# Attention beside routing: GpSimd's row transfers of a group dealt 5, 2 + 1 + 4 and 4 over three batches, and the first batch's matmuls in another order

## The chip, the cores and the metric

The kernel runs on one core of a Trainium2 chip. The core has TensorE (PE, matrix products into the eight PSUM banks), VectorE (DVE), ScalarE (ACT), GpSimd (POOL), SyncE (SP, which issues DMAs) and 16 DMA engines. Each engine takes its own instructions in order, and engines wait for one another by semaphores. The metric is the time of one execution in microseconds, the median over runs. The profile is of a single execution.

## The reference

One launch computes four residual blocks on 16 sequences of 256 tokens with 128 features:

```python
x = x + s4d_block(layernorm(x))      # long convolution by FFT, then a norm
x = x + mixture(layernorm(x))        # 8 experts, the best 2 of them, and a shared one; hidden 512
x = x + attention(layernorm(x))      # 16 heads of 8 features, causal, with a slope per head
x = x + mixture(layernorm(x))        # the same weights again

logits = q @ k.T * scale + slopes * (j - i);  masked to j <= i
out = softmax(logits) @ v @ Wout

logits = xf @ gate_w + gate_b;  top_w, top_i = top_k(logits, 2);  gw = softmax(top_w)
out = sum_e combine[:, e] * (gelu(xf @ w1[e] + b1[e]) @ w2[e] + b2[e]) + shared(xf)
```

## The kernel before

The kernel has four stages, with a barrier of all engines between them: the front (convolution, gating), the attention stage (which first finishes the experts of the first mixture), the shared expert of the second mixture, and the routed experts of it. The change touches the attention stage alone.

**The attention stage** works through 16 batches (sequences) of four quarters (`G` = 0 to 3, four heads each). Every engine has a function `quarter_of(b, G)`, called for all batches in order, so the order of each engine's work is written out by hand. A batch is spread over several steps: in step `b` TensorE computes the scores of batch `b` (`scores`, line 1994 and 1998, with masks on 1947), the maxima of batch `b + 1` (`maxima`, in two tiles, lines 1953 and 1970), the projections of `b + 3`, and the end of `b - 1` and `b - 2`. Quarters are numbered `x = 4 b + G`.

- `maxima(y, tile)` writes banks 2 and 3; VectorE reduces them (`reduce`, line 2227) before the next maxima may write them. The reduced rows are turned, copied by ScalarE (line 2145) and written into the query rows by small DMAs of SyncE (`spread_m`, line 1859). `scores` of quarter 0 and 2 wait for these.
- `scores(x)` writes banks 5 to 7 when the exponential before it is through (`exps`). ScalarE's `expo` (line 2150) reads them.
- `weigh(x)` (lines 2029, 2030) multiplies the exponentials with the values, into bank 4. `expo(x)` waits for `weigh(x - 2)`.
- In step 0 the last of the first mixture's rows come in (`middle`: ScalarE line 1697, turned by TensorE, line 1712).

**The second mixture's routing** runs beside it. When batch `c` is complete, VectorE takes its statistics (line 2249); GpSimd makes the mean and scale of them (`batches.statistics`, lines 1111 to 1121); ScalarE normalises in step `c + 3`, quarter 2, ahead of its exponential (line 1134); GpSimd splits the rows (`batches.rows`, lines 1126 and 1127), and SyncE turns them (line 1143). Four batches make a group of eight tiles of 128 rows. VectorE chooses the experts and places, and GpSimd sends each tile's rows to a DRAM buffer `slots` by indirect DMAs, one for each tile and choice: eight for the first choice (`dispatch_first`, line 1058), eight for the second (`dispatch_second`, line 1071), which first need the index column of the row rewritten (line 1067). Two groups are sent in this stage, group 0 in GpSimd's turns `c` = 7, 8, 9 and group 1 in 11, 12, 13; the other two are sent in the next stage. The second choice of a half (four tiles) waits until the first choice of that half has landed.

GpSimd's loop over `c` takes, in order, the statistics, the places (`place_on_pool`), the row split and the transfers. Its next turn's statistics stand behind these transfers.

Of the kernel before, what the change touches and what calls it, by code (L numbers as in the profile page):

```python
# [51 lines left out]
GRP = 8  # L52
# [1677 lines left out]
def attention_stage(nc, t):  # L1730
# [13 lines left out]
    with ExitStack() as ctx:  # L1744
# [50 lines left out]
        def after(eng, s, n):  # L1795

            if n > 0:
                eng.wait_ge(s, n)

        assert at[0] + ROUTE_WORDS <= ARENA - BACK_WORDS  # L1800
        route = route_program(nc, t, sem, t.arena[:, at[0]:])
# [3 lines left out]
        def batch(c):  # L1805
            return 0 <= c < NB

        def quarter(x):
            return 0 <= x < LAST
# [65 lines left out]
        @block.gpsimd  # L1875
        def _(pool):
            words = [v.rearrange("p s G n -> p (s G n)").bitcast(F32) for v in QPAD]
            for v in (*words, V32[0], V32[1], LATER_ROWS, EARLIER_ROWS, LATER, EARLIER):
                nc.gpsimd.memset(v, 0.0).then_inc(cleared, 1)
            pool.wait_ge(cleared, 9)  # L1880
            for v in V32:
                nc.gpsimd.memset(v[:, :, :, 8:9], 1.0).then_inc(masks, 1)

            for rows, base in ((LATER_ROWS, HALF), (EARLIER_ROWS, HALF - 1)):
                nc.gpsimd.affine_select(out=rows, in_=rows, compare_op=ALU.not_equal, fill=1.0, base=base,
                                        pattern=[[-1, 2 * P]], channel_multiplier=1).then_inc(masks, 1)

            nc.gpsimd.affine_select(out=LATER, in_=LATER, compare_op=ALU.is_ge, fill=-1.0e30, base=0,
                                    pattern=[[0, 2], [1, P]], channel_multiplier=-1).then_inc(masks, 1)

            nc.gpsimd.affine_select(out=EARLIER, in_=EARLIER, compare_op=ALU.is_ge, fill=-1.0e30, base=-1,
                                    pattern=[[0, 2], [-1, P]], channel_multiplier=1).then_inc(masks, 1)
            pool.wait_ge(masks, 6)
            for a in range(2):
                first, at_a = slice(HALF * a, HALF * a + 1), HALF * a
                nc.gpsimd.memset(LATER_ROWS[first, at_a + HALF:at_a + HALF + 1], 0.0).then_inc(masks, 1)
                nc.gpsimd.memset(LATER_ROWS[first, at_a + P:at_a + P + HALF], 1.0).then_inc(masks, 1)
                nc.gpsimd.memset(EARLIER_ROWS[first, at_a:at_a + HALF], 1.0).then_inc(masks, 1)
                nc.gpsimd.memset(LATER[first, :, at_a:at_a + HALF], -1.0e30).then_inc(masks, 1)
            pool.wait_ge(masks, 14)  # L1900
            routed.gpsimd(pool)
            for k in range(len(PIECES)):
                middle.root(pool, k)
            route.clear(pool)
            for c in range(NB - 1):
                pool.wait_ge(row_stats, c + 1)
                batches.statistics(pool, c)
                for g in range(SENT_IN_ATTENTION):
                    if c == 4 * g + 7:
                        route.place_on_pool(pool, g)  # L1910
                batches.rows(pool, c)
                for g in range(SENT_IN_ATTENTION):
                    if c == 4 * g + 7:
                        route.dispatch_first(pool, g, range(0, GRP // 2))
                    if c == 4 * g + 8:
                        route.dispatch_first(pool, g, range(GRP // 2, GRP))
                        route.dispatch_second(pool, g, (0,))
                    if c == 4 * g + 9:
                        route.dispatch_second(pool, g, (1,))
            route.sent_all(pool, SENT_IN_ATTENTION)  # L1920

        @block.tensor
        def _(pe):
# [20 lines left out]
            def mask_later(out, a, half, start):  # L1944

                first = HALF * (a + 1 - half)
                pe.matmul(out[:, :, HALF * half:HALF * half + HALF], LATER_ROWS[PAIR[a], first:first + P],  # L1947
                          LATER[PAIR[a], :, HALF * a:HALF * a + HALF], start=start, stop=False, skip_group_check=True)
# [33 lines left out]
            def scores(x):  # L1982

                c, G = divmod(x, HG)
                if G % 2 == 0:
                    pe.wait_ge(mrow_in[G // 2], 32 * (c + 1))
                if x == 0:
                    pe.wait_ge(middle.low, 4)
                after(pe, exps, x)
                early = [ps[5 + a].rearrange("p (h t n) -> p h t n", t=TPB, n=P)[:, :, 0] for a in range(2)]  # L1990
                late = [ps[7][:, SEQ * a:SEQ * a + SEQ].rearrange("p (h n) -> p h n", n=P) for a in range(2)]

                def early_scores(a):
                    return pe.matmul(ps[5 + a], KST[c % 3][PAIR[a], G, 0:P], QPAD[c % 3][PAIR[a], :, G, :], start=False,  # L1994
                                     stop=True, skip_group_check=True)

                def late_scores(a):
                    return pe.matmul(ps[7][:, SEQ * a:SEQ * a + SEQ], KST[c % 3][PAIR[a], G, P:2 * P],
                                     QPAD[c % 3][PAIR[a], :, G, P:2 * P], start=False, stop=True, skip_group_check=True)
                mask_later(late[0], 0, 0, True)  # L2000
                mask_later(early[1], 1, 0, True)
                mask_later(late[0], 0, 1, False)
                mask_later(early[1], 1, 1, False)
                late_scores(0).then_inc(st_mm, 1)
                early_scores(1)
                mask_later(early[0], 0, 0, True)
                mask_later(early[0], 0, 1, False)
                pe.wait_ge(st_mm, 3 * x + 1)
                mask_later(late[1], 1, 0, True)
                mask_later(late[1], 1, 1, False)  # L2010
                early_scores(0).then_inc(st_mm, 1)
                late_scores(1).then_inc(st_mm, 1)
# [44 lines left out]

            def quarter_of(b, G):
                x = HG * b + G
                if quarter(x):  # L2060
                    scores(x)
                if quarter(x + 4):
                    maxima(x + 4, 0)
                if quarter(x - 1):
                    weigh(x - 1)
                if G == 3:
                    if gate_group(b) is not None:
                        for c in range(4 * gate_group(b), 4 * gate_group(b) + 4):
                            batches.landed(pe, c)
                        after(pe, mrow_set, min(2 * b + 3, 2 * NB))  # L2070
                        route.gate(pe, gate_group(b), ps[0])
                    if rank_group(b) is not None:
                        after(pe, mrow_set, min(2 * b + 3, 2 * NB))
                        route.rank(pe, rank_group(b), ps[0])
                if quarter(x + 5):
                    maxima(x + 5, 1)
                if G == 0:
                    if batch(b - 2):
                        turn_out(b - 2)
                    if batch(b + 3):  # L2080
                        project(b + 3)
                if G == 1 and batch(b - 2):
                    project_out(b - 2)
                if G == 2:
                    if batch(b + 1):
                        pe.wait_ge(vset, b + 2)
                        turn_maxima(b + 1, 0)
                    if batch(b - 1):
                        turn_back(b - 1, 0)
                if G == 3:  # L2090
                    if batch(b + 1):
                        after(pe, mrow_set, 2 * b + 3)
                        if gate_group(b) is not None:
                            route.logits_taken(pe, gate_group(b))
                        if rank_group(b) is not None:
                            route.ranks_taken(pe, rank_group(b))
                        turn_maxima(b + 1, 1)
                    if batch(b - 1):
                        turn_back(b - 1, 1)
                if b == -1 and G == 0:  # L2100
                    middle.turn(pe, 2)
                    middle.turn(pe, 3)
                if b == 0:
                    middle.turn(pe, 4 + G)
                if G == 1 and batch(b + 1):
                    values(b + 1)

# [370 lines left out]
```

## Time and profile before

| | |
|---|---|
| median of 3 runs | 870.53 us (869.16 to 872.47) |
| the profiled execution | 869.57 us, span 867.8 us |
| busy: TensorE, VectorE, GpSimd, ScalarE | 616.0, 618.4, 458.5, 438.3 us |
| row transfers in all | 128 (64 of each choice), 32 of them in the attention stage |
| steps of batches 0 to 15 in attention | from 411.7 to about 625 us |

Times in the rows are from the span's start. The median of the runs is 0.96 us above the profiled execution's own time, and its span is 1.8 us below that. A row of windows gives the stretch and its length, then the busy time of TensorE (PE), its weight loads (PEld), VectorE, ScalarE and GpSimd with their instructions, the granted clock as a share of full speed, the share of the DMA engines' time and GB/s. A row of a timeline gives start, duration, engine, line, operation, result and operand with their shape. Where an engine's row ends in square brackets, it had stood idle for so long before it, and the bracket names what ended the wait.

### The profile page before, as it was taken

To read this page: it belongs to the slowest core of one execution; us is meant where nothing else is said; L and a number is where in the kernel's file an instruction comes from. 1 tells how busy PE (TensorE), PEld (TensorE's weight loads), DVE (VectorE), ACT (ScalarE), POOL (GpSimd) and SP (SyncE) were. 2 spreads that over 40 slices of the span, in tenths; PEclk is the share of its full clock that TensorE was granted. 3 is DMA by queue.
4 is the path that set the end of the run, shared out by engine and by line. 5 is a ranking of instruction groups with operands and counts; after the bars stand their busy time and mean duration, and the time that the engine had idled before them with its cause. 6 is when DMAs were issued, how large, how long until landed. Compare 5 with 4: busy or idle time off the path is not lost. (4 is left out here: it accounts for less than half of the span.)

```text
span 867.8 us, 21824 instructions
## 1 busy us (share of the span) xinstructions
PE 616.0 (71%) x7762; PEld 451.0 (52%) x7762; DVE 618.4 (71%) x1397; ACT 438.3 (51%) x873; POOL 458.5 (53%) x591
## 2 busy tenths in 40 slices
PE   0569975780079999225799999989714795999950
PEld 0354433560069999212566666555402574999940
DVE  6997887683048888287688889888513873888846
ACT  5634457760035555171766676666603332555524
POOL 1238758887547777510002223464764880777760
PEclk9968987995579999755899999999956997999985
DMA  9610002351144464242122233342111512545418
GB/s 284 151 38 1 0 8 67 71 90 50 37 74 90 98 99 88 86 166 62 45 87 71 80 98 88 82 116 55 42 33 29 86 32 47 93 101 100 89 32 285
DMA packets 131850, 70.51 MB, mean 81 GB/s; under 512 B 89535, under 2 KB 118725, under 8 KB 131746
## 3 DMA queue, kind: packets, MB, share of 16 engines
q1 hardware_dynamic: 121042, 50.46, 25.1%
q0 software_dynamic: 9088, 16.88, 7.0%
q10 hardware_dynamic: 1616, 1.77, 0.7%
q8 instruction: 67, 1.10, 0.5%
q14 instruction: 37, 0.30, 0.1%
HBM read 26.61 MB, written 30.50 MB: 66 GB/s over the span
## 5 line engine op out<-in xcount | busy, mean ns | idle before, releaser
L1500 ACT ACTIVATE ARENA<-banks,ARENA 128x256 f32<-128x256 f32 x312 | 122.3, 476 | 97.1 <-PE banks L1460 94.6
L2227 DVE TENSOR_REDUCE ARENA<-banks 128x4 f32<-128x1024 f32 (+1 forms) x128 | 122.8, 959 | 32.5 <-PE banks L1970 29.5
L1458 PE MATMUL banks<-ARENA,W1H 128*128 128x256 f16 x312 | 87.2, 279 | 58.4 <-DMA ARENA<-slots 57.6
L1472 PE MATMUL banks<-W2L,ARENA 128*128 x624 | 110.0, 219 | 2.7 <-DVE ARENA L1513 2.3
L1473 PE MATMUL banks<-W2H,ARENA 128*128 x624 | 109.7, 219 | 0.1
L1474 PE MATMUL banks<-W2H,ARENA 128*128 x624 | 109.7, 219 | 0.0
L2150 ACT ACTIVATE ARENA<-banks 128x1536 f32<-128x1536 f32 x64 | 92.6, 1447 | 24.2 <-PE banks L1994 24.1
L1448 POOL DMA_INDIRECT expert_out_g<-ARENA x78 | 78.0, 999 | 46.6 <-issue 26.2
L1448 POOL DMA_INDIRECT expert_out_f<-ARENA x78 | 81.1, 1040 | 33.6 <-issue 23.9
L1532 DVE TENSOR_TENSOR ARENA<-ARENA 128x1024 f16<-128x1024 f32 x78 | 95.6, 1226 | 2.7
L1058 POOL DMA_INDIRECT slots<-ARENA,PLACE x64 | 77.0, 1204 | 26.0 <-issue 17.5
L1071 POOL DMA_INDIRECT slots<-ARENA,PLACE x64 | 77.5, 1211 | 19.1 <-issue 14.6
L1459 PE MATMUL banks<-ARENA,W1H 128*128 128x256 f16 x312 | 87.1, 279 | 0.0
L1460 PE MATMUL banks<-ARENA,W1L 128*128 128x256 f16 x312 | 87.1, 279 | 0.0
L1530 DVE CAST ARENA<-ARENA 128x1024 f16<-128x1024 f32 x78 | 55.2, 707 | 37.1 <-ACT ARENA L1500 36.6
L1458 PEld LDWEIGHTS banks<-ARENA,W1H 128*128 x312 | 31.3, 100 | 63.5 <-issue 59.3
L1472 PEld LDWEIGHTS banks<-W2L,ARENA 128*128 128x128 f16 x624 | 61.0, 98 | 4.7 <-issue 3.7
L1473 PEld LDWEIGHTS banks<-W2H,ARENA 128*128 128x128 f16 x624 | 61.0, 98 | 1.8 <-issue 0.3
L1474 PEld LDWEIGHTS banks<-W2H,ARENA 128*128 128x128 f16 x624 | 61.0, 98 | 0.0
L488 PE MATMUL banks<-XN,ARENA 128*128 128x512 f32 x64 | 33.6, 685 | 34.0 <-ACT XN L395 29.6
L1953 PE MATMUL banks<-ARENA 64*128 64x128 bf16 x512 | 37.7, 227 | 20.9 <-DVE ARENA L2227 13.4
L1947 PE MATMUL banks<-ARENA 64*128 64x128 bf16 x512 | 47.4, 222 | 5.7 <-ACT ARENA L2150 3.7
(324 smaller groups left out, 1731.3 us busy)
## 6 DMA issues: line engine op xcount, KB each, us to landing
spread<-ARENA SPq DMA_DIRECT2D x96, 64.0 KB
ARENA<-expert_out_f SPq DMA_DIRECT2D x8, 512.0 KB, 6.5
ARENA<-spread SPq DMA_DIRECT2D x16, 256.0 KB, 3.0
ARENA<-spread SPq DMA_DIRECT2D x32, 128.0 KB, 2.8
ARENA<-expert_out_g SPq DMA_DIRECT2D x8, 512.0 KB, 6.6
XT<-in_w SPq DMA_DIRECT2D x10, 256.0 KB, 7.7
slots<-EMPTY SPq DMA_DIRECT2D x16, 129.0 KB
ARENA<-in_w SPq DMA_DIRECT2D x8, 256.0 KB, 6.9
```

What stands on the lines that cost most here:

```text
L1071: nc.gpsimd.indirect_dma_start(xs, bass.IndirectOffsetOnAxis(ap=t.PLACE[:, 1, i:i + 1], axis=0), ROWI[:, i, :], None).then_inc(sent[h], 16)
L1448: nc.gpsimd.indirect_dma_start(yo, bass.IndirectOffsetOnAxis(ap=target, axis=0), Y[i % 4][:, h], None, bounds_check=2 * NT * P - 1, oob_is ...
L1458: pe.matmul(out, t.W1H[:, e, ms], XST[i][:, 0], start=True, stop=False)
L1459: pe.matmul(out, t.W1H[:, e, ms], XST[i][:, 1], start=False, stop=False)
L1460: ins = pe.matmul(out, t.W1L[:, e, ms], XST[i][:, 0], start=False, stop=True)
L1472: pe.matmul(out, hh, t.W2L[:, e, m, :], start=(m == 0), stop=False)
L1473: pe.matmul(out, hh, t.W2H[:, e, m, :], start=False, stop=False)
L1474: ins = pe.matmul(out, hl, t.W2H[:, e, m, :], start=False, stop=(m == MT - 1))
L1500: ins = nc.scalar.activation(HF[i % 2][:, m], UP[i % 2][:, m], ACT.Gelu, bias=BIAS[i % 4][:, m:m + 1], scale=1.0 / WS)
L1532: dve.tensor_tensor(H16[i % 4][:, 1], HF[i % 2], H16[i % 4][:, 0], ALU.subtract).then_inc(split, 1)
L2150: nc.scalar.activation(PR[x % 2], t.psum_all[:, 5:8, :], ACT.Exp, scale=1.0 / LOGIT).then_inc(exps, 1)
L2227: dve.tensor_reduce(MX[:, G // 2, tile, :, :, G % 2].rearrange("p s a -> p a s"), src, AX.X, ALU.max).then_inc(m_red, 1)
```

## The change

GpSimd's eight first-choice transfers of a group were dealt four and four over two turns, each after the row split, and the second choices four and four over the second and third turn. Now the first turn sends five; the second sends two between the statistics and the row split, one after the row split, and then the second choices of the first half; the third turn is as before.

On TensorE, in the steps up to batch 0 (`full` is false), a quarter begins with the first maxima and only then computes the scores, and the weighting of the quarter before comes at the end, before the values. From batch 1 on the order is the old one.

```diff
                 for g in range(SENT_IN_ATTENTION):
                     if c == 4 * g + 7:
                         route.place_on_pool(pool, g)
+                    if c == 4 * g + 8:
+                        route.dispatch_first(pool, g, range(5, 7))
                 batches.rows(pool, c)
                 for g in range(SENT_IN_ATTENTION):
                     if c == 4 * g + 7:
-                        route.dispatch_first(pool, g, range(0, GRP // 2))
+                        route.dispatch_first(pool, g, range(0, 5))
                     if c == 4 * g + 8:
-                        route.dispatch_first(pool, g, range(GRP // 2, GRP))
+                        route.dispatch_first(pool, g, range(7, GRP))
                         route.dispatch_second(pool, g, (0,))
                     if c == 4 * g + 9:
                         route.dispatch_second(pool, g, (1,))
...
                 x = HG * b + G
-                if quarter(x):
+                full = b > 0
+                if full and quarter(x):
                     scores(x)
                 if quarter(x + 4):
                     maxima(x + 4, 0)
-                if quarter(x - 1):
+                if not full and quarter(x):
+                    scores(x)
+                if full and quarter(x - 1):
                     weigh(x - 1)
...
                 if b == 0:
                     middle.turn(pe, 4 + G)
+                if not full and quarter(x - 1):
+                    weigh(x - 1)
                 if G == 1 and batch(b + 1):
                     values(b + 1)
```

On GpSimd, at the first group's turns 7 and 8, the difference reads as follows (1058 is a first-choice transfer, 1111 and on the statistics, 1126 and 1127 the row split):

```order
-L1058 DMA slots<-ARENA,PLACE 36608x129 x4
...
-L1126 CAST ARENA<-XN 128x2x128
-L1127 TENSOR_TENSOR ARENA<-XN,ARENA 128x2x128
-L1058 DMA slots<-ARENA,PLACE 36608x129 x4
+L1058 DMA slots<-ARENA,PLACE 36608x129 x5
...
+L1121 TENSOR_SCALAR NRM<-NRM 128x2
+L1058 DMA slots<-ARENA,PLACE 36608x129 x2
+L1126 CAST ARENA<-XN 128x2x128
+L1127 TENSOR_TENSOR ARENA<-XN,ARENA 128x2x128
+L1058 DMA slots<-ARENA,PLACE 36608x129
```

Four transfers moved: one into the turn before, two ahead of the row split, and one stays behind it; the four second choices follow as they did.

On TensorE, batch 0, from the turn of the late rows that ends quarter 2 (line 1712) into quarter 3, before:

```order
L1712 MATMUL banks<-ID,XN 128x128 x4
L1947 MATMUL banks<-ARENA 128x2x64 x4
L1998 MATMUL banks<-ARENA 128x256
L1994 MATMUL banks<-ARENA 128x512
...
L1953 MATMUL banks<-ARENA 128x2x64 x4
L1970 MATMUL banks<-ARENA 128x128 x4
L2029 MATMUL banks<-ARENA 32x256
L2030 MATMUL banks<-ARENA 32x128
...
L1953 MATMUL banks<-ARENA 128x2x64 x4
L1970 MATMUL banks<-ARENA 128x256 x4
```

and now (its line numbers are two higher):

```order
L1712 MATMUL banks<-ID,XN 128x128 x4
L2031 MATMUL banks<-ARENA 32x256
L2032 MATMUL banks<-ARENA 32x128
...
L1955 MATMUL banks<-ARENA 128x2x64 x4
L1972 MATMUL banks<-ARENA 128x128 x4
L1949 MATMUL banks<-ARENA 128x2x64 x4
L2000 MATMUL banks<-ARENA 128x256
L1996 MATMUL banks<-ARENA 128x512
...
L1955 MATMUL banks<-ARENA 128x2x64 x4
L1972 MATMUL banks<-ARENA 128x256 x4
```

The weighting of quarter 1 (2029, 2030) stood ahead of the second maxima of quarter 2 and now closes quarter 2; the one of quarter 2, shown in the first block, moves behind the second maxima of quarter 3; and the first maxima (1953, 1970 at 128x128) stand ahead of the scores.

## Rows read from the trace of the kernel before

**Rows 1.** The page, the chain that ended last: shares of the span.

```profile
POOL 7%; issue 5%; DVE 2%; DMA 1%; ACT 0%; POOLq 0%; PE 0%; SPq 0%; DVEq 0%; ACTq 0%
```

**Rows 2.** Windows, first exponential to first exponential: batches 8, 10 and 12.

```profile
522.10:534.84 12.74, 12.56 (x208) 7.87 (x210) 11.71 (x28) 9.05 (x14) 3.70 (x13) 1.00 0.30 85
...
547.96:561.93 13.97, 12.45 (x210) 7.88 (x204) 10.98 (x22) 9.05 (x14) 9.16 (x23) 1.00 0.35 99
...
575.40:589.86 14.46, 12.27 (x204) 7.67 (x200) 11.30 (x27) 9.04 (x13) 10.74 (x21) 1.00 0.38 107
```

**Rows 3.** Timeline of GpSimd: start, duration, engine, line, operation.

```profile
566.28 0.22 POOL L1121 TENSOR_SCALAR NRM<-NRM 128x2 f32<-128x2 f32 x1
568.83 0.40 POOL L1126 CAST ARENA<-XN 128x256 f16<-128x256 f32 x1 [2.33 <-ACT XN L1134]
...
570.25 1.09 POOL L1058 DMA_INDIRECT slots<-ARENA,PLACE  x1 [0.29 <-POOL ARENA L1127]
571.65 0.95 POOL L1058 DMA_INDIRECT slots<-ARENA,PLACE  x1 [0.31 <-issue]
...
580.38 0.21 POOL L1111 TENSOR_TENSOR NRM<-RSTATS 128x2 f32<-128x2 f32 x1
```

**Rows 4.** Timelines of ScalarE and TensorE in batch 12.

```profile
581.09 0.38 ACT L2139 ACTIVATE ARENA<-banks 128x256 f32<-128x256 f32 x1 [0.89 <-PE banks L1941]
583.69 0.88 ACT L1134 ACTIVATE XN<-RES,NRM 128x128 f32<-128x128 f32 x2 [2.21 <-POOL NRM L1121]
...
585.95 0.29 PE L1947 MATMUL banks<-ARENA 64*128 64x128 bf16 x4 [1.98 <-ACT ARENA L2150]
```

**Rows 5.** Timelines of SyncE's DMA issues and of TensorE's first scores.

```profile
531.58 3.57 SPq L1859 DMA_DIRECT2D ARENA<-ARENA  x4
553.75 3.82 SPq L1842 DMA_DIRECT2D spread<-ARENA  x6
557.62 3.21 SPq L1859 DMA_DIRECT2D ARENA<-ARENA  x4
566.86 4.24 SPq L1842 DMA_DIRECT2D spread<-ARENA  x6
580.36 4.62 SPq L1842 DMA_DIRECT2D spread<-ARENA  x6
586.18 3.98 SPq L1859 DMA_DIRECT2D ARENA<-ARENA  x4
...
533.92 0.29 PE L1947 MATMUL banks<-ARENA 64*128 64x128 bf16 x4
561.01 0.29 PE L1947 MATMUL banks<-ARENA 64*128 64x128 bf16 x4 [1.34 <-DMA ARENA<-ARENA]
588.95 0.29 PE L1947 MATMUL banks<-ARENA 64*128 64x128 bf16 x4
```

**Rows 6.** Timelines of GpSimd and VectorE at the end of the stage.

```profile
615.53 0.20 POOL L1111 TENSOR_TENSOR NRM<-RSTATS 128x2 f32<-128x2 f32 x1
619.69 0.40 POOL L1126 CAST ARENA<-XN 128x256 f16<-128x256 f32 x1 [0.98 <-ACT XN L1134]
631.23 0.21 POOL L1111 TENSOR_TENSOR NRM<-RSTATS 128x2 f32<-128x2 f32 x1
646.69 0.65 POOL L1127 TENSOR_TENSOR ARENA<-XN,ARENA 128x256 f16<-128x256 f32 x1
...
625.70 0.48 DVE L2249 BATCH_NORM_STATS2 RSTATS<-RES 128x6 f32<-128x128 f32 x2
```

**Rows 7.** TensorE in batch 0, and a window with the granted clock.

```profile
420.08 0.28 PE L1953 MATMUL banks<-ARENA 64*128 64x128 bf16 x4 [1.00 <-DVE ARENA L2227]
425.78 0.28 PE L1978 MATMUL banks<-ID,ARENA 128*16 128x128 f16 x2 [1.78 <-ACT ARENA L2139]
427.12 0.29 PE L1947 MATMUL banks<-ARENA 64*128 64x128 bf16 x4 [0.47 <-ACT ARENA L2150]
...
427.00:429.00 2.00, 1.88 (x24) 1.29 (x28) 0.97 (x2) 1.77 (x5) 0.00 (x0) 0.59 0.01 2
```

## The prediction

> **What bounds the kernel now.** I read the page first, then the attention stage (409 to 652 us) batch by batch, because both edits lie there. The chain that ended last [rows 1] is GpSimd's issue of the last mixture's results; it starts only at 723.6 us, so an earlier end of what lies before it moves it whole. I follow a batch by the start of its first exponential. An undisturbed batch lasts 12.74 us, with TensorE busy for 12.56 of it; batch 10 lasts 13.97 and batch 12 14.46, both at the full clock, with TensorE busy for about as long as ever [rows 2]. So TensorE, in a tight exchange with VectorE and ScalarE, is the bound, and these two batches hold waits.
>
> *Batch 12's wait.* GpSimd issues eight row transfers in batch 11, from 570.25 us, and can begin the statistics of batch 9 only when they are out, at 580.38; they take 3.3 us [rows 3]. ScalarE stood idle 2.21 us before normalising with them: it was free at 581.48 (581.09 + 0.39) and started at 583.69. The exponential behind it came late, and TensorE's next scores waited 1.98 us for that [rows 4].
>
> *Batch 10's wait.* The scores that open a batch need the row of maxima, which SyncE writes with small DMAs. In a quiet batch SyncE begins these at 531.58 and the scores start at 533.92, 2.34 us later. Where four row transfers have been going out since 556.28, SyncE begins at 557.62 and the scores start at 561.01, 3.39 us later, 1.34 of it an idle wait for that DMA [rows 5]. In batch 12 transfers and SyncE's DMAs went out together, from 586.2, and the scores started at 588.95 without a wait: the ScalarE stall had given the DMA time [rows 5].
>
> *The end of the stage.* From 615.53 to 647.34 us GpSimd never waits for VectorE: it is behind. Batch 12's statistics follow the transfers without idle, and batch 13's start at 631.23 though VectorE had finished its part at about 626.1 (625.70, two of 0.24). Its only idle there is 0.98 us for ScalarE's normalisation, ahead of each pair of row copies; the last copy ends at 647.34, its transposes follow, and then all engines meet [rows 6].
>
> **Part 1: the dealing, first group (batches 10 to 12).** A transfer costs 0.95 us and 0.30 until the next, 1.26 in step, and 1.39 for the first after other work [rows 3]. Five instead of four: the fourth ended at 560.21 + 0.95 = 561.16, the fifth at 562.42, before the next statistics at 563.32: covered by 0.9 us. Then two ahead of the row copies: statistics end at 566.50; two take 0.29 + 1.09 + 0.30 + 0.96 = 2.64, to 569.14. The copies started at 568.83, so they are 0.35 late (their transposes were issued at 575.81, so nothing waits). One more and four: copies end 570.3, the single transfer at 571.7, the counter 0.15, and four at 5.1 end at 576.95. That is 3.4 us sooner than 580.37. Batch 9's statistics, whose input came at 576.72, then end at 580.2, 1.3 us before ScalarE wants them. ScalarE's wait of 2.21 goes, and with it TensorE's of **1.98 us** [rows 4].
>
> What is late next: the DMA of the maxima. Without the stall TensorE would want to open batch 13 at 588.95 − 1.98 = 586.97. SyncE cannot begin these DMAs before its stores are through: 580.36 + 4.62 = 584.98, perhaps 0.3 sooner [rows 5]. By the quiet distance they land at about 587.0 (584.65 + 2.34), by batch 10's at 588.4 (584.98 + 3.39). So the gain lies between 588.95 − 588.4 = 0.55 and 1.95. The second half's transfers now go out from 583.8 (ScalarE done at 582.35, copies 1.13 and gaps), ahead of SyncE's DMAs as in batch 10, so I take a value near that row: **−0.9 us**.
>
> The two moved transfers leave at 566.8, beside SyncE's stores (566.86), where before there were none. Stores took 3.82 us in batch 10 without transfers beside them and 4.62 in batch 12 with them [rows 5]. If 0.4 of it appears in batch 11, the maxima's DMAs start at 571.5 and by batch 10's distance land at 574.9, against scores that started at 574.49: between 0 and 0.8 lost; I take **+0.3**. The Trainium skill (DMA: Bandwidth & Descriptors, Queues, rings and completion order) says each DMA engine takes turns, a packet at a time, between the queues that have work; by that rule the moved transfers do slow the stores, and the sum would stand by the upper of these bounds; the 1.34 us wait of batch 10 agrees with it.
>
> **Part 2: the dealing, second group (batches 14 to 16).** Counted along GpSimd from the end of batch 11's copies, 610.34. Before: statistics of batch 13 at 631.23. Now: five transfers end at 616.76; statistics 3.18, to 619.97; two transfers, 2.64, to 622.6, in which ScalarE's normalisation (0.88) is done, so that the idle of 0.98 is filled; copies 1.13, to 623.8; one, to 625.2; counter and four, 5.3, to 630.4. **−0.8 us** (between −0.5 and −0.98), straight through to the end of the stage. What it makes late: ScalarE's normalisation of batch 12 stands ahead of the exponentials of batch 15 in its queue and now waits 1.26 us for statistics that end at 619.97 instead of 618.71; TensorE's and VectorE's tail slips by as much, and batches 13's and 14's inputs come at 627.4 and 632.1. GpSimd wants them at 630.4 and about 641.2, so this is covered by 3 us and 9 us. Were GpSimd not behind, it would cost 1.26.
>
> **Part 3: the ramp (batch 0).** No instruction is added. In quarter 0 the first maxima waited for VectorE (reduce over at 412.73) and the scores ran in that gap. Now the maxima start at the same 412.78, and the scores (1.08 us at the low clock) fill the gap behind; the next maxima start 0.05 late. The exponential waits for ScalarE until 415.16 either way. In quarter 1 the exponential comes 0.35 late, but VectorE's queue sets the pace: TensorE waited 1.00 for it at 420.08 [rows 7] and still will. In quarter 2 TensorE idled 1.78 us until ScalarE's values at 425.78, then 0.47 until 427.12. The weighting (0.87 at full clock) that ran ahead of that gap now runs after it, closing the second gap and costing about 0.4; quarter 3's scores start near 427.9, 0.8 late, while the last maxima start at about 429.2 rather than 430.04. The weighting of quarter 2 goes behind them. Batch 1's first scores then start at about 431.7, where they stood at 431.59, and VectorE's next reduce, at 432.93, is held by its own queue. TensorE waited 0.21 at 433.67, which takes up that difference. **0.0 us**, between −0.5 and +0.8. Much of this runs at the low granted clock (0.59 over 427 to 429, where 0.50 is the low level) [rows 7]; that this stays so is an assumption.
>
> **Sum.** −0.9 + 0.3 − 0.8 + 0.0 = −1.4. Against the profiled execution's own 869.57 us (span 867.8) that is 868.2. The three runs have a median of 870.53, 0.96 above it, so against them it is 869.1. I state **869.1**.
>
> **The rivals.**
> *All of the stall comes back.* The maxima land as in a quiet batch and the stores are not slowed: −1.98 − 0.8 = −2.8, 867.7. For it: in batch 12 the scores followed 2.77 after SyncE's start with transfers beside them, less than 3.39. Against it: they will again be ahead of SyncE's DMAs. 0.2.
>
> *DMA takes all of the middle.* The landing takes 3.39 in batch 13 (−0.55) and batch 11 loses 0.8: +0.25, with the tail −0.8: −0.55, 870.0. For it: batch 10's row. Against it: both at their worst. 0.2.
>
> *The ramp costs clock: slower.* With the weighting moved, TensorE idles from 418.3 to 420.1 instead of 419.07 to 420.08, and longer ahead of 425.78. A stretch at the low of its two levels (0.50 of full, 1.2 instead of 2.4 GHz) like that from 427.2 to 430.8 (about 3.6 us) holds TensorE back by 1.8. It decides if more than 2.8 us of low clock fall on work that TensorE bounds, behind 427; two such stretches cost 3.6, net +2.2: 872.7. For it: TensorE had been idle most of 423 to 427 before that fall. Against it: the same idle is there now and led to one stretch alone. 0.12. The Trainium skill (TensorE: Matmul & The Clock Gate, The HAM clock gate) says that the throttled state is the default and sustained activity releases it, at a phase that the kernel does not set; by that rule such a stretch may come in one run and not in another, and the time would be this rival's.
>
> *The ramp gains.* The last maxima of quarter 3, 0.8 earlier, carry through, and the low stretch shrinks: −1.0 more, −2.4: 868.1. 0.06.
>
> *Something downstream shifts by more than 4.35 us*, either way, such as the second mixture's transfers meeting other work: nothing in the rows speaks for it. 0.05.
>
> My own forecast has 0.37.
>
> **How the numbers follow.** The four smaller cases lie between 867.7 and 872.7. The three runs of before alone spread from 869.16 to 872.47. With the ends of the first three parts (−1.95 − 0.98 − 0.5 = −3.4, and −0.55 + 0.8 − 0.5 + 0.8 = +0.55) from 870.53, the forecast spans 867.1 to 871.1; the run's own scatter widens it, and the slow rival is let in at the top: 866.0 to 872.5. 0.5% is 4.35 us, about what a measurement of this kernel can tell from none; no case but the last reaches it, so same holds 0.89, faster 0.07 (the full gain and scatter together), slower 0.04.
>
> **What would show it.** ScalarE's 2.2 us idle before batch 12's normalisation gone, and GpSimd's statistics there ending near 580 (on before's clock); in its place a wait of TensorE for the maxima's DMA at batch 13, 1.2 us by my sum, none by the first rival, 1.5 by the second. Batch 12 between 12.5 and 13.9 us long. In the tail a new wait of ScalarE for GpSimd of about 1.2 us, and the time from batch 11's last row copy to batch 13's statistics 20.1 us instead of 20.9. Batch 1's first exponential within 0.5 us of where it stood from the first maxima of the stage. I am wrong if GpSimd's fifth transfer delays batch 8's statistics, if the ramp is off by over 1 us, or if the stage ends earlier without the end moving.

## The result and the profile after

The changed kernel takes 868.05 us (median of 20 runs) against 870.75 for the kernel before (20 runs beside them): a ratio of 0.9968 [0.9956, 0.9981], or 2.8 us less (1.7 to 3.8). One run of each kernel was far slower than the rest (1112.31 us of the changed one, 1538.46 of before) and is left out of the ratio. The profiled execution took 867.45 us, its span 865.6, where before it was 869.57 and 867.8. I had forecast −1.4 us, and one of the rivals −2.8.

**The middle.** Windows from first exponential to first exponential, batches 8, 10 and 12, columns as in [rows 2]:

```profile
522.90:535.79 12.89, 12.63 (x212) 8.02 (x212) 11.84 (x29) 9.04 (x14) 3.71 (x13) 1.00 0.30 84
549.36:561.92 12.56, 12.38 (x206) 7.72 (x202) 10.55 (x20) 9.04 (x13) 8.52 (x23) 1.00 0.36 101
575.46:588.18 12.72, 12.45 (x210) 7.89 (x204) 11.82 (x28) 9.04 (x13) 8.86 (x20) 1.00 0.39 111
```

Batch 12 fell from 14.46 to 12.72 us, as short as an undisturbed one. Batch 10 is shorter here too, but over the experiments' profiles it comes long or short with either dealing. GpSimd's timeline of the turns in question:

```profile
562.86 0.96 POOL L1058 DMA_INDIRECT slots<-ARENA,PLACE  x1 [0.31 <-issue]
563.84 0.21 POOL L1111 TENSOR_TENSOR NRM<-RSTATS 128x2 f32<-128x2 f32 x1
...
567.52 1.08 POOL L1058 DMA_INDIRECT slots<-ARENA,PLACE  x1 [0.50 <-issue]
568.90 0.96 POOL L1058 DMA_INDIRECT slots<-ARENA,PLACE  x1 [0.30 <-issue]
569.87 0.41 POOL L1126 CAST ARENA<-XN 128x256 f16<-128x256 f32 x1
...
580.55 0.22 POOL L1121 TENSOR_SCALAR NRM<-NRM 128x2 f32<-128x2 f32 x1
```

The fifth transfer ends at 563.82 and the statistics begin at 563.84; two transfers follow, and the next statistics end at 580.77. In [rows 3] they only began at 580.38. ScalarE and TensorE in the same batch, against [rows 4]:

```profile
581.15 0.38 ACT L2146 ACTIVATE ARENA<-banks 128x256 f32<-128x256 f32 x1 [0.88 <-PE banks L1943]
581.43 0.87 ACT L1134 ACTIVATE XN<-RES,NRM 128x128 f32<-128x128 f32 x2
...
587.27 0.29 PE L1949 MATMUL banks<-ARENA 64*128 64x128 bf16 x4
```

Both waits, 2.21 us on ScalarE and 1.98 on TensorE, are gone. The last row is the opening of batch 13, where I expected a new wait of 1.2 us for the maxima's DMA: there is none. SyncE's issues, against [rows 5]:

```profile
580.43 4.13 SPq L1842 DMA_DIRECT2D spread<-ARENA  x6
584.60 3.88 SPq L1859 DMA_DIRECT2D ARENA<-ARENA  x4
```

**The end of the stage.** GpSimd and ScalarE, against [rows 6]:

```profile
614.92 0.20 POOL L1111 TENSOR_TENSOR NRM<-RSTATS 128x2 f32<-128x2 f32 x1
628.65 0.20 POOL L1111 TENSOR_TENSOR NRM<-RSTATS 128x2 f32<-128x2 f32 x1
644.09 0.65 POOL L1127 TENSOR_TENSOR ARENA<-XN,ARENA 128x256 f16<-128x256 f32 x1
656.66 0.71 POOL L1205 TENSOR_TENSOR NRM<-NRM,MHALF 128x2 f32<-128x2 f32 x1 [11.91 <-DVE NRM L86]
657.86 1.09 POOL L1058 DMA_INDIRECT slots<-ARENA,PLACE  x1 [0.29 <-POOL ARENA L940]
...
618.13 0.88 ACT L1134 ACTIVATE XN<-RES,NRM 128x128 f32<-128x128 f32 x2 [1.29 <-POOL NRM L1121]
```

The stage's last row copy ends at 644.74 instead of 647.34, and the next stage's first transfer starts 13.1 us behind it in both (before at 660.46). That 2.6 us reaches the end but for 0.4: the span is 2.2 shorter. ScalarE's new wait of 1.29 is there as forecast.

**The ramp.** TensorE's waits in batch 0 and the windows with the granted clock (the column ahead of the last two), against [rows 7]:

```profile
419.31 0.29 PE L1955 MATMUL banks<-ARENA 64*128 64x128 bf16 x4 [2.54 <-DVE ARENA L2234]
425.02 0.36 PE L1980 MATMUL banks<-ID,ARENA 128*16 128x128 f16 x2 [1.71 <-ACT ARENA L2146]
...
425.00:427.00 2.00, 1.98 (x14) 1.25 (x18) 0.00 (x0) 2.00 (x3) 0.00 (x0) 0.52 0.11 32
427.00:429.00 2.00, 2.00 (x35) 1.24 (x25) 1.20 (x2) 0.44 (x2) 0.00 (x0) 0.63 0.02 4
429.00:431.00 2.00, 1.86 (x26) 1.10 (x26) 1.65 (x4) 1.74 (x3) 0.00 (x0) 1.00 0.00 0
```

The 0.47 wait of [rows 7] is closed, but the wait for VectorE in quarter 1 (419.31) is 2.54 us where it was 1.00, and the stretch at the low level came about 2 us earlier.

### The profile page after: what moved, and what is told of

Same layout as the page of the kernel before. It is cut to its first block and busy times, and to the rows that moved or that the text cites. A ratio compares the mean times of both kernels' runs of the same rounds, so it can differ in the third digit from the quotient of the medians.

```text
span 865.6 us, 21826 instructions
## 1 busy us (share of the span) xinstructions
PE 615.8 (71%) x7762; PEld 452.5 (52%) x7762; DVE 619.1 (72%) x1397; ACT 437.7 (51%) x873; POOL 459.1 (53%) x591
## 5 line engine op out<-in xcount | busy, mean ns | idle before, releaser
L1955 PE MATMUL banks<-ARENA 64*128 64x128 bf16 x512 | 37.4, 226 | 23.0 <-DVE ARENA L2234 15.2
L1111 POOL TENSOR_TENSOR NRM<-RSTATS 128x2 f32<-128x2 f32 x15 | 3.0, 199 | 91.8 <-DVE RSTATS L2256 91.7
```

## The experiments

Edits are shown against the changed kernel. In the third to the ninth run, batch 0 also has its old order (`full = True`); the two repeats at the end are unedited. "Batch 12" is the time from its first exponential to batch 13's; "the tail" is the time on GpSimd from the end of batch 11's row copy to batch 13's statistics (20.89 us before, 20.19 after).

### One part at a time

**The dealing without the ramp.**

```diff
-                full = b > 0
+                full = True
```

> The new dealing of both groups, with the old order in batch 0. Theory A (the dealing carries all of it: the 1.98 us stall of batch 12 comes back whole and the end of the stage gives 0.7): 2.7 us faster than before, 3.1 if the ramp costs the 0.4 that the trace shows. Theory B (my forecast: the landing of the maxima rows takes half of the stall back): 1.4 us faster. Theory C (the ramp gains): less than 2.7. In the profile by A batch 12 lasts 12.7 us and no wait for the maxima rows opens batch 13.

Measured: 0.9967 [0.9950, 0.9984]: the whole change's value. Batch 12 lasts 13.26 us, the tail 20.23. The landing shows here, and it is short. TensorE's opening of batch 13 in this run, and SyncE's issue for it:

```profile
585.98 3.07 SPq L1859 DMA_DIRECT2D ARENA<-ARENA  x4
...
588.37 0.29 PE L1949 MATMUL banks<-ARENA 64*128 64x128 bf16 x4 [0.47 <-DMA ARENA<-ARENA]
```

588.37 − 585.98 = 2.39 us, the quiet distance, although GpSimd's transfers go out beside it.

**The ramp without the dealing.**

```diff
-                    if c == 4 * g + 8:
-                        route.dispatch_first(pool, g, range(5, 7))
...
-                        route.dispatch_first(pool, g, range(0, 5))
+                        route.dispatch_first(pool, g, range(0, GRP // 2))
-                        route.dispatch_first(pool, g, range(7, GRP))
+                        route.dispatch_first(pool, g, range(GRP // 2, GRP))
```

> The new order in batch 0 alone, the old dealing. The forecast's term: 0.0, between 0.5 faster and 0.8 slower. Theory A: 0.4 us slower, as the first exponential of batch 1 stood 0.4 us further from the first maxima. Theory C (the ramp gains part of the 2.7): 1 us faster or more. The 2.2 us wait of ScalarE for GpSimd in batch 12 stays in the profile.

Measured: 1.0001 [0.9986, 1.0017]: nothing, as summed. Yet in this execution the clock did not fall a second time in the ramp; the same stretch as shown above for the changed kernel:

```profile
425.00:427.00 2.00, 1.91 (x37) 1.18 (x36) 0.72 (x2) 1.53 (x5) 0.00 (x0) 1.00 0.00 0
427.00:429.00 2.00, 1.28 (x18) 0.82 (x20) 1.65 (x4) 1.80 (x2) 0.00 (x0) 1.00 0.02 4
```

Batch 1's second exponential came 23.31 us after ScalarE's first normalisation of eight tiles at the head of the stage, against 24.14 in the changed kernel's profile. In the changed kernel's repeat (below), which has such a stretch too, it is 23.76. So the low stretch is worth some 0.4 to 0.8 us, and executions of the same code in the ramp differ by it.

**The dealing of one group alone.** First group 0 (batches 10 to 12), then group 1 (the tail); shown for group 0.

```diff
-                    if c == 4 * g + 8:
+                    if c == 4 * g + 8 and g == 0:
...
-                        route.dispatch_first(pool, g, range(0, 5))
+                        route.dispatch_first(pool, g, range(0, 5 if g == 0 else 4))
-                        route.dispatch_first(pool, g, range(7, GRP))
+                        route.dispatch_first(pool, g, range(7 if g == 0 else 4, GRP))
```

> The new dealing of group 0 alone (batches 10 to 12), the rest as before. Theory A: 2.0 us faster, ScalarE's wait for GpSimd gone, batch 12 some 1.7 us shorter, and the end of the stage as before (20.9 us from the last row copy of turn 11 to the statistics of turn 13). Theory B: 0.6 us faster, with a wait of 1.2 us for the maxima rows at batch 13.

> The new dealing of group 1 alone (batches 14 to 16). Both theories: GpSimd bounds the end of the stage, so 0.7 to 0.8 us faster, 20.1 us instead of 20.9 from the last row copy of turn 11 to the statistics of turn 13, with a new wait of ScalarE for GpSimd of 1.2 us that costs nothing. Rival (TensorE's tail bounds the end): 1.2 us slower. ScalarE's wait of 2.2 us in batch 12 stays.

Measured: group 0 0.9972 [0.9955, 0.9988], −2.4 us; group 1 0.9988 [0.9972, 1.0004], −1.0, which the interval does not tell from nothing; the two add up to a little more than both together (−2.9). In the traces the tail is 20.18 us with group 1 dealt. With group 0, batch 12 lasts 13.26 and its landing wait is 0.46. In the run with group 1 alone the old stall of batch 12 is still there, and something stood behind it that the profile of before had not shown: the batch lasts 15.98 us instead of 14.46. ScalarE's and TensorE's rows, and the granted clock:

```profile
585.28 0.88 ACT L1134 ACTIVATE XN<-RES,NRM 128x128 f32<-128x128 f32 x2 [2.20 <-POOL NRM L1121]
587.54 0.29 PE L1949 MATMUL banks<-ARENA 64*128 64x128 bf16 x4 [1.98 <-ACT ARENA L2157]
589.90 0.63 PE L1972 MATMUL banks<-ARENA 64*128 64x256 f16 x4
...
584.00:587.00 3.00, 1.54 (x27) 0.67 (x16) 2.56 (x6) 1.72 (x3) 1.77 (x5) 1.00 0.43 124
...
588.00:590.00 2.00, 2.00 (x36) 1.29 (x36) 1.18 (x4) 1.46 (x2) 1.70 (x2) 0.73 0.12 37
590.00:592.00 2.00, 2.00 (x20) 0.94 (x14) 1.39 (x2) 0.37 (x1) 1.39 (x3) 0.50 0.10 33
```

The waits are those of [rows 4], but TensorE, busy for 1.54 of the 3 us around the stall, was then granted the low of its two levels (0.50, 1.2 GHz instead of 2.4): the maxima's four matmuls of 256 columns took 0.63 us instead of 0.38, and the batch grew by 1.5 us. In the profile of before, TensorE was busy for 1.55 of the same 3 us, counted from the stall's end (582.41 to 585.41), and the clock stayed at full, so these rows don't tell why it fell here and not there.

### Fewer or smaller steps

**Five, then three behind the row split**: the two transfers ahead of the split go behind it.

```diff
-                    if c == 4 * g + 8:
-                        route.dispatch_first(pool, g, range(5, 7))
...
-                        route.dispatch_first(pool, g, range(7, GRP))
+                        route.dispatch_first(pool, g, range(5, GRP))
```

> Both groups dealt 5, 3 + 4, 4, nothing ahead of the row split; old order in batch 0. GpSimd then ends batch 11's seven transfers about 1.3 us sooner than with eight, so batch 9's statistics end 0.8 to 0.9 us after ScalarE is free: its wait shrinks from 2.2 to about 0.9 us, and the end of the stage stays at 20.9 us, as the idle of 0.98 us ahead of the split stays. Theory A (the two ahead of the split matter): 1.3 us faster than before, 1.5 us behind the whole dealing. Rival (any shortening is enough): as fast as the whole dealing, 2.8 us.

Measured: 0.9960 [0.9947, 0.9974], −3.5 us where 1.3 was expected. ScalarE's rows at batches 12 and 15:

```profile
583.72 0.88 ACT L1134 ACTIVATE XN<-RES,NRM 128x128 f32<-128x128 f32 x2 [0.83 <-POOL NRM L1121]
...
620.21 0.88 ACT L1134 ACTIVATE XN<-RES,NRM 128x128 f32<-128x128 f32 x2 [1.28 <-POOL NRM L1121]
```

A wait of 0.83 us is left, and TensorE's behind it is 0.61; but batch 12, at 13.13 us, is no longer than the others of the new dealing. The tail is 20.88, the old value. So in the middle one transfer less before batch 9's statistics is enough; the rest of the wait covers only the time until the maxima land (batch 13's scores followed 2.33 us after SyncE's start, the quiet distance). The total rests on five runs. That it comes out better than the whole dealing, which has the tail's 0.7 us besides, is not shown: the intervals overlap.

**Four, then two ahead of the split**: the fifth transfer stays in the second turn.

```diff
-                        route.dispatch_first(pool, g, range(5, 7))
+                        route.dispatch_first(pool, g, range(4, 6))
...
-                        route.dispatch_first(pool, g, range(0, 5))
+                        route.dispatch_first(pool, g, range(0, 4))
-                        route.dispatch_first(pool, g, range(7, GRP))
+                        route.dispatch_first(pool, g, range(6, GRP))
```

> Both groups dealt 4, 2 + 2 + 4, 4; old order in batch 0. The two ahead of the row split start inside GpSimd's idle of 2.3 us, so the eight transfers end 2.1 us sooner than before; batch 9's statistics end about when ScalarE is free. Theory A: ScalarE's wait in batch 12 under 0.3 us, the end of the stage 20.1 us from row copy to statistics, 2.5 us faster than before, so that the fifth transfer in the turn before buys nothing. Rival (the fifth is needed): 1.5 us or less.

Measured: 0.9953 [0.9937, 0.9969]. Batch 12 is 12.94 us with a wait of 0.29 on ScalarE, the tail 20.18, and ScalarE's 1.3 us wait in the tail is absent. The fifth transfer buys nothing that can be measured: either edit that brings the statistics forward by over a microsecond takes batch 12 to the length of the new dealing, and the tail's 0.7 us belongs to the pair ahead of the split. That this smaller change, too, comes out below the full one is inside the intervals.

### The tail

GpSimd is behind at the end of the stage, so I tried to fill its remaining idle with the last four second choices, now issued by a new function `dispatch_half` (not shown), which sends given tiles of one half. First moved behind the last row copy, then partly into the idle, then all into it in pairs; shown for the last:

```diff
+                last = SENT_IN_ATTENTION - 1
+                if c == 4 * last + 9:
+                    route.dispatch_half(pool, last, 1, (0, 1))
+                if c == 4 * last + 10:
+                    route.dispatch_half(pool, last, 1, (2, 3))
                 batches.rows(pool, c)
...
-                    if c == 4 * g + 9:
+                    if c == 4 * g + 9 and g < last:
                         route.dispatch_second(pool, g, (1,))
```

> The whole dealing, old order in batch 0, and besides, group 1's last four transfers go behind the last row split. Theory A (GpSimd bounds the end of the stage, then the transposes of the last split): the last split comes 5.2 us sooner and its transposes run beside the four transfers; the next stage begins 2 to 3 us sooner than with the dealing alone, 5 us faster than before in all (0.994). Rival (something else ends the stage, or the next stage gives it back): as the dealing alone, 0.997.

> As the last one, but one of the four transfers goes ahead of the row split in each of the last two turns, into GpSimd's two idle times of 0.98 us, and two behind the last split. Theory A: the idle times go, the stage ends another 1 to 1.8 us sooner, 6 to 7 us faster than before (0.992). Rival (the transposes of the last split end the stage and come 0.8 us later): 4 us faster, behind the last one.

> The whole dealing, old order in batch 0, and group 1's last four transfers in pairs ahead of the row splits of the last two turns, none behind the last. From the last row copy of turn 11 the dealing alone reached the next stage's first transfer in 49.4 us, 13.1 of it behind the last copy; with transfers last it was 14.5 behind them. Theory A (GpSimd's own work bounds the end; filled idle counts whole, and the stage must not end with transfers): 47.4 us, 2 us less than the dealing alone, 4.7 us faster than before (0.9945). Rival (the pairs delay the splits by as much as they fill): 49.4 and 0.997.

Measured: all four last 0.9979 [0.9966, 0.9992]; one ahead of each pair of copies and two last 0.9960 [0.9944, 0.9977]; in pairs 0.9942 [0.9919, 0.9965], as expected, and the lowest ratio of all versions (866.16 us against 871.64 beside it), though it rests on six runs and its interval overlaps that of the changed kernel, so the gain over it is shown by the traces and not by the total. The first two expectations failed: 0.994 and 0.992 were both too much. From batch 11's row copies to the next stage's first transfer it was 49.4 us in the changed kernel, 50.8 with all four last, 48.9 with two last and 47.6 in pairs. GpSimd's rows with all four last, and in pairs:

```profile
640.48 0.40 POOL L1126 CAST ARENA<-XN 128x256 f16<-128x256 f32 x1 [0.98 <-ACT XN L1134]
646.04 0.96 POOL L1071 DMA_INDIRECT slots<-ARENA,PLACE  x1 [0.30 <-issue]
661.50 1.04 POOL L1058 DMA_INDIRECT slots<-ARENA,PLACE  x1 [0.29 <-POOL ARENA L940]
```

```profile
634.94 0.96 POOL L1084 DMA_INDIRECT slots<-ARENA,PLACE  x1 [0.30 <-issue]
635.90 0.41 POOL L1141 CAST ARENA<-XN 128x256 f16<-128x256 f32 x1
...
641.87 0.96 POOL L1084 DMA_INDIRECT slots<-ARENA,PLACE  x1 [0.30 <-issue]
...
643.33 0.65 POOL L1142 TENSOR_TENSOR ARENA<-XN,ARENA 128x256 f16<-128x256 f32 x1
657.34 1.05 POOL L1058 DMA_INDIRECT slots<-ARENA,PLACE  x1 [0.29 <-POOL ARENA L940]
```

With all four last, GpSimd ends at 647.00 with as much work and idle as in the changed kernel (36.3 us from batch 11's row copy in both), and 14.5 us pass to the next stage's first transfer; with a row copy last, 13.1 to 13.4. Putting the transfers in pairs where it idled 0.98 us takes those waits out. What bounds this tail is the sum of GpSimd's work and idle, not the row copies.

### The repeats

> The whole change again, beside the others on one chip: 2.7 us faster than before by all theories. By theory A batch 12 lasts 12.7 to 13.3 us here as in every run with the new dealing, and by theory B a wait for the maxima rows of 0.5 us or more opens batch 13.

> The kernel before, profiled again, for what differs from one execution to the next. Theory A: batch 12 lasts 14.3 us or more, with ScalarE's wait of 2.1 to 2.2 us, and GpSimd needs 20.9 us from the last row copy of turn 11 to the statistics of turn 13; batches 6 and 10 take anything between 12.5 and 14.2 us by when the maxima rows land, whatever the dealing.

Measured: the changed kernel again 0.9968 [0.9953, 0.9984]; the kernel before, a single run, 872.46 us with a span of 870.6. In the latter batch 12 lasts 15.94 us, with a wait of 2.38 on ScalarE and the clock at 0.50 over 590 to 592: the second of the four profiles with the old dealing of group 0 to hold such a fall (14.46, 14.32, 15.98, 15.94 us). In the changed kernel's repeat, batch 12 lasts 12.84 at the full clock, but a clock fall stands elsewhere, behind a 1.59 us wait for the maxima in batch 10:

```profile
562.62 0.35 PE L1949 MATMUL banks<-ARENA 64*128 64x128 bf16 x4 [1.59 <-DMA ARENA<-ARENA]
...
560.00:562.00 2.00, 1.03 (x12) 0.47 (x12) 1.65 (x5) 0.54 (x2) 1.39 (x3) 1.00 0.39 110
562.00:564.00 2.00, 1.38 (x20) 1.13 (x20) 0.22 (x1) 0.08 (x1) 1.49 (x2) 0.68 0.29 72
564.00:566.00 2.00, 2.00 (x28) 1.00 (x26) 1.08 (x3) 1.37 (x1) 0.48 (x3) 0.50 0.28 66
```

## Why the prediction was right in direction and half in size

**The base of the sum was right**: batches 10 and 12 and GpSimd's lateness in the tail were the places, and the traces show the mechanism of part 1 and part 2 row by row. The rival that gives all of the stall back, 867.7 against 868.05 measured, is the case that came. What it is made of is not quite what it said, as the third point shows.

**The step that failed: "I take a value near that row: −0.9 us".** I read batch 10's 3.39 us from SyncE's start to the scores as the distance when transfers stand ahead, and expected batch 13 to be like it. The runs show 2.39 to 2.53 there (waits of 0.45 to 0.47 in four profiles), and in the changed kernel the scores followed 587.27 − 584.60 = 2.67 after SyncE's start without a wait. And 2.9 to 3.6 us are seen in batch 5, where GpSimd issues no transfer at all: the changed kernel's opening of batch 6 and SyncE's issue for it,

```profile
492.55 3.37 SPq L1859 DMA_DIRECT2D ARENA<-ARENA  x4
...
496.00 0.28 PE L1949 MATMUL banks<-ARENA 64*128 64x128 bf16 x4 [1.23 <-DMA ARENA<-ARENA]
```

are 3.45 apart, and all thirteen profiles but that of before have such a long batch 5 (13.7 to 14.1 us against 12.56). Batch 10 was long in six of thirteen profiles, with either dealing. One row had served as a law, and the cause that it was put down to, the transfers, is not what makes the distance long.

What does go with it is the batch and the time. Every wait for the maxima in another of batches 3 to 12 ended 2.33 to 2.53 us after SyncE's start. In batches 5 and 10 TensorE waited whenever SyncE started 9.45 us or more behind the batch's first exponential (18 cases), and then the scores opened only at 12.8 to 13.3; where SyncE started at 9.31 or earlier (8 cases), they opened at 11.65 without a wait. Batch 10 in the changed kernel is such a case (558.41 − 549.36 = 9.05), and in [rows 5] it is one of the others (557.62 − 547.96 = 9.66). These two batches also share something that no other batch has at this place, in all thirteen profiles: a packet of the DMA queue q14, of the kind "instruction", starts 11.2 to 11.8 us behind the first exponential. In before it starts at 559.31, in the changed kernel at 560.73, where batch 11 opens so:

```profile
558.41 3.82 SPq L1859 DMA_DIRECT2D ARENA<-ARENA  x4
...
561.00 0.29 PE L1949 MATMUL banks<-ARENA 64*128 64x128 bf16 x4
```

That this packet is what holds a late landing back is not shown, since no run moved it; that batch 12, which has none, can't be priced by batch 10 is.

**The term that was mis-sized: the stall itself.** Over the profiles, batch 12 lasts 15.2 us with the old dealing (four) and 13.0 with the new (nine, from 12.7 to 13.3): −2.1, not −0.9. Of that, 1.3 is the wait: the two old batches without a clock fall last 14.4 us. It is less than TensorE's waits in these two (1.98 and 1.80) because the new batches keep something of their own: waits of 0.45 to 0.47 for the landing in four of the nine and of 0.61 for ScalarE in one, and some 0.3 on average that no wait accounts for. The rest is the clock: in two of four executions the stall brought TensorE down to the low level for some 3 us, 1.5 us each time. My base, one profile, had missed it. The Trainium skill (TensorE: Matmul & The Clock Gate, The HAM clock gate) says the throttled state is the default and sustained activity releases it; I had used this for the ramp alone, and these rows agree with it for the stall, in some executions and not in others. No profile with the new dealing shows a fall in batch 12.

**The moved transfers, +0.3.** Batch 11 lasts 13.4 us with the old dealing (13.1 to 13.7) and 13.7 with the new (13.3 to 14.1, one of the nine holding part of a clock fall), the size forecast, though the two overlap so far that the difference may be scatter. But the stated cause is not there: SyncE's six stores of batch 11 take 4.07 to 4.27 us without the transfers beside them (four profiles) and 3.83 to 4.54 with (eight), the same on average (4.19 and 4.19). The forecast had priced them by 3.82 in batch 10 and 4.62 in batch 12; but the six stores of batch 9, ahead of all of these transfers, took 4.4 to 5.2 us in the thirteen profiles, so such a length is no sign of transfers. The rule that I cited for it (DMA: Bandwidth & Descriptors, of the Trainium skill) is not contradicted, since it says nothing of how long an issue takes; its effect is just not seen in these rows. What makes the 0.2 or 0.3, if it is there, stays open.

**The tail, −0.8**: 20.89 to 20.19, −0.7, in every run with the pair ahead of the split, and ScalarE's new wait of 1.29 cost nothing. In the middle the fifth transfer ends where the sum put it, 14.46 us after batch 10's first exponential (563.82 − 549.36; forecast 562.42 − 547.96). Its cover of 0.9 us was counted in a batch 10 of 13.97 us; with one of 12.56 it is used up, and the statistics start right behind the transfer. No later wait shows it.

**The ramp, 0.0**: alone 1.0001. Batch 1's first exponential stands 20.65 us behind that normalisation with the new order (three profiles), 20.33 with the old (ten); the second one 23.7 and 23.6. The mean hides two states: all ten profiles with the old order have the low stretch, and of the three with the new order two have it (24.14 and 23.76) and one has not (23.31). With the stretch in both, the new order is some 0.3 us slower; whether it makes the stretch rarer, three profiles can't tell. The assumption that the low stretch stays where it was failed: it came earlier or not at all.

**The sum from the runs**: −2.1 + 0.3 − 0.7 + 0.1 = −2.4, against −2.8 (1.7 to 3.8) measured.

## What to carry to other kernels

A wait on the path can cost more than its length when the engine behind it is TensorE: in some executions the clock falls behind it, and one profile may be the lucky one, so look at a second before pricing the wait. A distance read once (an issue to its landing) is one draw; look for it in stretches where the supposed cause is absent before it stands for that cause, and see at what time in the batch it starts. And where an in-order engine is behind at the end of a stage, its work plus its idle sets the end: put independent issues into its waits, in the order that leaves none.

## What the runs showed of the hardware

In the stage behind attention, GpSimd's transfers, 0.96 us elsewhere, take up to 2.86 us beside VectorE's long operations that have both inputs in SBUF (line 1318). The changed kernel's timelines of GpSimd and VectorE:

```profile
664.32 1.38 POOL L1058 DMA_INDIRECT slots<-ARENA,PLACE  x1 [0.30 <-issue]
666.00 2.74 POOL L1058 DMA_INDIRECT slots<-ARENA,PLACE  x1 [0.30 <-issue]
...
664.33 1.24 DVE L1316 CAST ARENA<-ARENA 128x2048 f16<-128x2048 f32 x1 [5.33 <-ACT ARENA L1282]
665.61 2.29 DVE L1318 TENSOR_TENSOR ARENA<-ARENA 128x2048 f16<-128x2048 f32 x1
```

The second transfer began 0.39 us into the 2.29 us operation and ended 0.84 us behind it, so nearly all of its usual 0.96 us came after. The Trainium skill (SBUF — State Buffer, Who interferes with whom) says that only the port pair shared by VectorE and GpSimd causes contention, as an exclusive lock; the rows agree, though no run here separates it from other causes.
